# Second layer of a two-layer transformer kernel: sums loaded in halves, a half-precision slot map, the attention's queries and angles put ahead of the expert beats, the gates applied in the last additions

## The chip, the cores and the metric

The kernel runs on one core of one Trainium2 chip. The metric is the device time of one execution in microseconds. The engines are TensorE (PE, with its weight load PEld), VectorE (DVE), ScalarE (ACT), GpSimd (POOL) and the DMA queues, of which SyncE's (SP) is the main one.

## The reference

Two layers on 4 sequences of 256 tokens with 256 features (1024 tokens, 8 tiles of 128). Each layer adds its attention and its mixture of experts to the residual. The change is nearly all in the second layer:

```python
# layer 1 attention: q, k with rotary turn, then random features of the unit vectors
qp = _softmax_kernel(q, rand_matrix)      # sin and cos of angles, 16 heads
kp = _softmax_kernel(k, rand_matrix)      # 8 heads, each used twice
kv = jnp.einsum('bhsf,bhsd->bsfd', kp, v) # sum over heads h, per token s
out = jnp.einsum('bhsf,bsfd->bhsd', qp, kv)
out = out.reshape(b, s, HID)              # not transposed: heads and tokens are mixed
return out @ Wo.T + bo
# layer 1 experts: 8 experts, the best 2 for each token
top_k_weights, top_k_indices = jax.lax.top_k(gate_logits, TOP_K)
h = jax.nn.silu(h0) * h1 * combine_w[..., None]
out = jnp.einsum('bsem,emd->bsd', h, wo)
```

## The kernel before, in words

Every engine has its own program, written out by hand, and the programs meet in semaphores only. Nothing is scheduled by a tool: what stands in a row on an engine runs in that row.

The first layer ends with its attention's last projection on PE (`project`) and two arrays of expert sums in DRAM. **The seam** between the layers: SP loads the sums (`SUMS`), DVE adds them to the residual `x3` (`add_sums`), takes the statistics, POOL makes the reciprocal root (`layernorm_pool`) and DVE the normed tokens (`layernorm_dve`). PE transposes them (`turn_tokens`), and ACT copies them out (`take_tokens`).

**The routing stage.** PE computes values and router logits (`values_router`), and queries and keys (`queries_keys`, six matmul groups of 512 columns). DVE picks the best two experts (`choose_dve`), turns the queries (`rope_qk`), counts (`route_dve_slots`, with `rank_pe` on PE), and builds the slot map: which token stands in which of the 23 tiles of 128 slots (`map1_dve`, 16 matmuls in `map1_pe`, `map1_dve_end`). Once the map is there (`map_ok`), POOL gathers the tokens of a tile by indirect DMA (`gather_tile1`). Beside this PE makes the angles of the random features (`angles`, `turn_angles`), and DVE and ACT norms, turns, differences, sines and squares of them.

**The beats.** Beat i on PE (`expert1_pe`) transposes gathered tile i, multiplies tile i-2 by the experts' first matrices, transposes the hidden tile i-4 and multiplies tile i-5 by the second. ACT copies and takes the silu (`expert1_act`), DVE multiplies (`middle`), POOL writes the rows back to DRAM (`write_tile1`). Between its `middle`s DVE does the attention's heads in 24 parts: `meet(t, part)`, three parts for each of 8 tiles. SP stores each finished tile of heads and loads it back in another order.

**The tail.** PE transposes the loaded heads (`turn_heads`), ACT copies (`take_heads`), PE projects (`project1`), DVE adds (`take_project1`). Then the expert rows come back from DRAM (`load_rows1`, rows of the first choice on SP's queue, of the second on ACT's) and DVE adds them, and SP writes the result.

Waits have the form `engine.wait_ge(semaphore, count)`. `NT` is 8 tiles, `NT1` 23, `NSL` 16, `B` 4 sequences, `TPB` 2 tiles of each.

## Time and profile before

| | us |
|---|---|
| median of 3 runs (528.59 to 534.28) | 533.49 |
| the profiled execution | 531.84 |
| its span | 530.0 |
| PE busy (share of the span) | 492.1 (93%) |
| DVE busy | 357.5 (67%) |
| ACT busy | 299.6 (57%) |
| POOL busy | 303.5 (57%) |

The span counts from the first to the last instruction; the execution's own time is 1.84 us longer. A share is a mean over stages: the second layer, which the change is about, takes the last 140 us. Its stages have to be read one by one.

### The profile page before, as it was taken

To read this page: it belongs to the slowest core of one execution; us is meant where nothing else is said; L and a number is where in the kernel's file an instruction comes from. 1 tells how busy PE (TensorE), PEld (TensorE's weight loads), DVE (VectorE), ACT (ScalarE), POOL (GpSimd) and SP (SyncE) were. 2 spreads that over 40 slices of the span, in tenths; PEclk is the share of its full clock that TensorE was granted. 3 is DMA by queue.
4 is the path that set the end of the run, shared out by engine and by line. 5 is a ranking of instruction groups with operands and counts; after the bars stand their busy time and mean duration, and the time that the engine had idled before them with its cause. 6 is when DMAs were issued, how large, how long until landed. Compare 5 with 4: busy or idle time off the path is not lost. (4 is left out here: it accounts for less than half of the span.)

```text
span 530.0 us, 9787 instructions
## 1 busy us (share of the span) xinstructions
PE 492.1 (93%) x2935; PEld 356.9 (67%) x2935; DVE 357.5 (67%) x1030; ACT 299.6 (57%) x667; POOL 303.5 (57%) x231
## 2 busy tenths in 40 slices
PE   8999799989799999999999999999979979899982
PEld 7666676778577777778777778786665535466661
DVE  6999735847767475576484681615477979999645
ACT  1256076687685776765766756747312358466530
POOL 1046447887877678576686786744133065788440
PEclk9999799999899999999999999999999999999998
DMA  7991738999779978588686796863669021444437
GB/s 222 330 365 36 206 100 190 201 205 276 185 172 287 223 169 193 100 192 191 133 209 136 151 228 151 186 111 31 171 200 309 15 69 61 99 117 108 86 81 236
DMA packets 92996, 89.20 MB, mean 168 GB/s; under 512 B 28273, under 2 KB 87793, under 8 KB 92561
## 3 DMA queue, kind: packets, MB, share of 16 engines
q1 hardware_dynamic: 73440, 59.25, 38.9%
q0 software_dynamic: 17376, 27.24, 27.2%
q10 hardware_dynamic: 2128, 2.10, 1.2%
q8 instruction: 24, 0.39, 0.3%
q14 instruction: 28, 0.22, 0.1%
HBM read 65.42 MB, written 21.29 MB: 164 GB/s over the span
## 5 line engine op out<-in xcount | busy, mean ns | idle before, releaser
L987 POOL DMA_INDIRECT expert_sums<-expert_weights,token_of_slot x79 | 131.5, 1665 | 60.8 <-ACT expert_weights L1097 32.7
L979 POOL DMA_INDIRECT expert_weights<-normed_x,token_of_slot x79 | 91.1, 1153 | 40.2 <-issue 17.9
L581 PE MATMUL bank<-out_weights,expert_weights 128*128 128x256 f32 x256 | 60.2, 381 | 0.7 <-ACT expert_weights L707 0.7
L581 PEld LDWEIGHTS bank<-out_weights,expert_weights 128*128 128x128 f32 x256 | 46.5, 190 | 8.0 <-ACT expert_weights L707 1.8
L1021 PEld LDWEIGHTS bank<-expert_weights 128*128 128x128 f32 x316 | 39.4, 191 | 11.1 <-issue 7.9
L1021 PE MATMUL bank<-expert_weights 128*128 128x128 f32 x316 | 43.8, 281 | 2.6 <-DMA expert_weights<-experts_in 2.0
L1320 PE MATMUL bank<-expert_weights,tiles 128*128 x92 | 44.1, 602 | 1.3 <-DVE tiles L1370 1.3
L1284 POOL DMA_INDIRECT tiles<-normed_x,token_of_slot x23 | 27.5, 1194 | 29.8 <-DVE token_of_slot L1278 20.5
L1043 PE MATMUL bank<-expert_weights 128*128 128x256 f32 x158 | 43.2, 392 | 0.7 <-ACT expert_weights L1074 0.7
L820 DVE SCALAR_TENSOR_TENSOR expert_weights<-bank,blocks_valid 128x64 f32<-128x64 f32 x32 | 7.2, 224 | 50.3 <-ACT expert_weights L684 49.1
L1289 POOL DMA_INDIRECT expert_rows<-expert_weights,token_of_slot x23 | 30.1, 1311 | 18.9 <-ACT expert_weights L1365 14.3
L1097 ACT ACTIVATE expert_weights<-bank,chosen_bf 128x256 f32<-128x256 f32 x79 | 33.3, 474 | 9.5 <-PE bank L1050 7.9
L1081 ACT ACTIVATE expert_weights<-bank,expert_weights 128x128 f32<-128x128 f32 x79 | 25.0, 370 | 17.5 <-PE bank L1021 17.3
L538 PE MATMUL bank<-keys,expert_weights 128*128 128x112 f32 x256 | 34.7, 279 | 0.0
L995 DVE SCALAR_TENSOR_TENSOR expert_weights<-expert_weights,chosen_before_bf 128x6 f32<-128x6 f32 x79 | 15.6, 222 | 28.0 <-DMA expert_weights<-normed_x,token_of_slot 28.0
L1088 ACT ACTIVATE expert_weights<-bank,expert_weights 128x128 f32<-128x128 f32 (+1 forms) x40 | 14.9, 372 | 34.7 <-PE bank L1031 32.5
L538 PEld LDWEIGHTS bank<-keys,expert_weights 128*128 128x128 f32 x256 | 31.1, 192 | 4.3 <-issue 4.3
L573 PE MATMUL bank<-expert_weights 112*128 112x512 f32 x64 | 33.0, 602 | 0.5 <-issue 0.3
L1043 PEld LDWEIGHTS bank<-expert_weights 128*128 128x128 f32 x158 | 27.9, 194 | 8.2 <-issue 3.6
L361 POOL TENSOR_TENSOR expert_weights<-iota,block_max 128x474 f32<-128x474 f32 x8 | 9.5, 1189 | 34.8 <-DVE block_max L347 30.1
L669 ACT ACTIVATE tiles<-bank 128x512 f32<-128x512 f32 x32 | 19.2, 601 | 17.8 <-PE bank L506 17.7
L1074 ACT ACTIVATE expert_weights<-bank 128x512 f32<-128x512 f32 (+1 forms) x40 | 24.0, 600 | 7.7 <-PE bank L1010 7.7
(282 smaller groups left out, 1124.5 us busy)
## 6 DMA issues: line engine op xcount, KB each, us to landing
expert_weights<-experts_in SPq DMA_DIRECT2D x79, 177.5 KB
expert_weights<-experts_out SPq DMA_DIRECT2D x79, 128.0 KB
expert_weights<-experts_rest SPq DMA_DIRECT2D x79, 64.2 KB
expert_weights<-L_ffn_wi SPq DMA_DIRECT2D x32, 128.0 KB
expert_weights<-w_comp SPq DMA_DIRECT2D x1, 2048.0 KB, 12.0
expert_weights<-fold_g SPq DMA_DIRECT2D x1, 2048.0 KB, 15.1
expert_sums<-zeros SPq DMA_DIRECT2D x2, 1024.0 KB, 21.1
expert_weights<-L_ffn_wo SPq DMA_DIRECT2D x16, 128.0 KB
```

The lines of the kernel that those rows point to most:

```text
L538: ins = nc.tensor.matmul(ps[2][:, hg * NKEY:(hg + 1) * NKEY], QT[:, s * H * NSR + hg * P:s * H * NSR + (hg + 1) * P], kwin[:, b, i, :], st ...
L573: nc.tensor.matmul(ps[out_bank(t, s)][:, :], VW[b % 2][0:NKEY, i * D:(i + 1) * D], PTB[s % 2][0:NKEY, :], start=True, stop=True).then_inc( ...
L581: ins = nc.tensor.matmul(ps[7][:, 0:HID], AO[:, h * P:(h + 1) * P], wc3[:, h, :], start=(h == 0), stop=(h == H - 1))
L979: nc.gpsimd.indirect_dma_start(xt0[g % 4], None, xn0, bass.IndirectOffsetOnAxis(ap=MAP[:, g:g + 1], axis=0)).then_inc(gathered[g % 4], 16)
L987: nc.gpsimd.indirect_dma_start(sums0[g % 2], bass.IndirectOffsetOnAxis(ap=MAP[:, g:g + 1], axis=0), yt0[g % 4], None, compute_op=ALU.add). ...
L1021: ins = nc.tensor.matmul(ps[5][:, g % 2 * P:(g % 2 + 1) * P], w1t[g % NW][:, k * W1C:k * W1C + P], xT0[q % 2][:, c * P:(c + 1) * P], start ...
L1043: nc.tensor.matmul(ps[YBANK[g % 2]][:, HID:2 * HID], hT0[q % 2][:, g % 2 * P:(g % 2 + 1) * P], w2t[q % NPT][:, g % 2 * HID:(g % 2 + 1) * H ...
L1081: ins = nc.scalar.activation(hT0[q % 2][:, c], ps[5][:, c], ACT.Relu, bias=w1t[g % NW][:, KC * W1C:])
L1097: nc.scalar.activation(yt0[g % 4], ps[YBANK[g % 2]][:, HID:2 * HID], ACT.Copy, scale=GY[:, g:g + 1]).then_inc(y_sb, 3 - len(pair(q)))
L1284: nc.gpsimd.indirect_dma_start(xt1[g % 4], None, xn1, bass.IndirectOffsetOnAxis(ap=MAPX1[:, g:g + 1], axis=0)).then_inc(gathered[n % 4], 16)
L1289: nc.gpsimd.indirect_dma_start(rows1, bass.IndirectOffsetOnAxis(ap=MAP[:, g:g + 1], axis=0), yt1[g % 4], None).then_inc(written1[g % 4], 16)
L1320: ins = nc.tensor.matmul(ps[HB[g % 2]][:, :], xT1[g % 3][:, k * P:(k + 1) * P], w[:, 0, k * 2 * MI:(k + 1) * 2 * MI], start=(k == 0), stop ...
```

## The change

- The sums of the first layer are loaded in four halves, and the first four tiles are normed before the rest has its statistics. Transposing tokens and `values_router` alternate on PE.
- In both layers, the comparison with the chosen experts and the product with the ranks are one DVE instruction each for all tiles, where there was one for each tile.
- The slot map of layer 1 is in half precision, without the gates, and 23 columns wide. The gates now multiply in the last additions on DVE (one instruction for each tile and choice).
- The second half of queries and keys has three PSUM banks of its own, so that PE needs no `rope_qk` before it. `map1_pe` follows the first `angles`, and `map1_dve_end` is two `rope_qk` instructions earlier than it was.
- In the beats, the head parts of DVE come one beat later than before and catch up (`PARTS1`); norms and turns of the second half are spread out; sines follow a table (`SINES1`). The addition of the output bias on POOL moves from ahead of the gathers to behind the sixth.
- Heads of two sequences are transposed inside the beats (`HEADS1`). The rows of both choices are loaded on SP's queue, by sequence, in a layout in which a partition's two tiles are adjacent in DRAM.

```diff
+HEADS1 = {NT1 + 1: 0, NT1 + 3: 1}
+SINES1 = {3: 1, 6: 2, 9: 3, 12: 4, 15: 5, 17: 6, 20: 7}
+PARTS1 = [g + (g >= 16) + (g >= 20) for g in range(NT1)]
...
-                st(nc.vector.tensor_tensor(oh[:, t], bc(IOTA[:, 0:E].unsqueeze(1), [P, K, E]),
-                                           bc(tf[:, t, 0:K].unsqueeze(2), [P, K, E]), ALU.is_equal))
-            st.wait()
+            n = hi - lo
+            st.link(nc.vector.tensor_tensor(oh[:, lo:hi], bc(IOTA[:, 0:E].unsqueeze(1).unsqueeze(1), [P, n, K, E]),
...
-                st(nc.vector.tensor_tensor(pr[:, t], oh[:, t],
-                                           bc(CUM[:, t * E:(t + 1) * E].unsqueeze(1), [P, K, E]), ALU.mult))
-            st.wait()
+            st.link(nc.vector.tensor_tensor(pr, oh, bc(v3(CUM[:, 0:NT * E], NT).unsqueeze(2), [P, NT, K, E]), ALU.mult))
...
-        MA1 = WC[:, NT * HID:NT * HID + NSL * P]
-        MT1, MTG1 = AO[:, 0:NSL * NT1], AO[:, NSL * NT1:3 * NSL * NT1]
-        MTGW = AO[:, NSL * NT1:3 * NSL * NT1 + P]
...
+        MA1 = WC[:, NT * HID:NT * HID + NSL * P // 2].bitcast(F16)
+        MT1, MTK1 = AO[:, 0:NSL * NT1], AO[:, NSL * NT1:NSL * NT1 + NSL * NT1 // 2].bitcast(F16)
...
-        QKB, ANGB, VRB, HB = (3, 5, 0), (4, 6, 0, 7), (2, 4, 6), (3, 5)
+        QKB, ANGB, VRB, HB = ((3, 5, 0), (7, 4, 6)), (4, 6, 0, 7), (2, 4, 6), (3, 5)
...
-            wait(pe, qk_rp, 2 * (i - NQK + 1))
-            pe.wait_ge(x1t_sb, NT // 2 * (hf + 1))
+            pe.wait_ge(x1t_sb, NT)
+            if hf == 1:
+                if c == 0:
+                    pe.wait_ge(op_sb, NT)
+                else:
+                    pe.wait_ge(vr_ok, c + 1)
...
-                ins = nc.tensor.matmul(ps[2][:, MAPC:MAPC + P], MA1[:, j * P:(j + 1) * P], MTGW[:, j * 2 * NT1:j * 2 * NT1 + P],
+                ins = nc.tensor.matmul(ps[2][:, MAPC:MAPC + NT1], MA1[:, j * P:(j + 1) * P], MTK1[:, j * NT1:(j + 1) * NT1],
...
-                nc.scalar.activation(yt1[g % 4], ps[1][:, 0:HID], ACT.Copy, scale=GY1[:, g:g + 1]).then_inc(y_sb, 1)
+                nc.scalar.activation(yt1[g % 4], ps[1][:, 0:HID], ACT.Copy).then_inc(y_sb, 1)
...
+            for t in range(1, NT - 1):
                 turn_tokens(pe, t)
-            for t in range(NT - 1):
-                values_router(pe, t)
+                values_router(pe, t - 1)
             turn_tokens(pe, NT - 1)
+            values_router(pe, NT - 2)
+            values_router(pe, NT - 1)
             queries_keys(pe, 0, 0)
-            values_router(pe, NT - 1)
             queries_keys(pe, 0, 1)
+            rank_pe(pe, E1, ps[2], 1)
             queries_keys(pe, 0, 2)
             queries_keys(pe, 1, 0)
-            rank_pe(pe, E1, ps[2], 1)
             queries_keys(pe, 1, 1)
-            pe.wait_ge(op_sb, NT)
+            queries_keys(pe, 1, 2)
             angles(pe, 0)
-            queries_keys(pe, 1, 2)
-            pe.wait_ge(vr_ok, 3)
+            map1_pe(pe)
             turn_angles(pe, 0)
             turn_angles(pe, 1)
-            map1_pe(pe)
             angles(pe, 1)
             expert1_pe(pe, 0, {})
+            expert1_pe(pe, 1, {})
             pe.wait_ge(slots_ok, 3)
-            expert1_pe(pe, 1, {})
-            turn_angles(pe, 2)
-            turn_angles(pe, 3)
             pe.wait_ge(ld_e1, 16 * 3 * KC * E1)
             for i in range(2, NBEAT1):
                 if i % 4 == 2:
                     e = experts1(pe, i)
                 expert1_pe(pe, i, e)
-            turn_heads(pe, 0)
+                if i == 2:
+                    turn_angles(pe, 2)
+                    turn_angles(pe, 3)
+                if i in HEADS1:
+                    turn_heads(pe, HEADS1[i])
             for b in range(B):
-                if b + 1 < B - 1:
-                    turn_heads(pe, b + 1)
-                elif b == B - 1:
-                    turn_heads(pe, b)
                 project1(pe, b)
-
...
+                for k in range(K1):
+                    sp.dma_start(v3(ROWS1[k], NT)[:, b * TPB:(b + 1) * TPB, :],
+                                 rows1[k * T:(k + 1) * T, :].rearrange("(p t) d -> p t d", t=NT)[:, b * TPB:(b + 1) * TPB, :]).then_inc(sum1_ld[b], 16)
...
+            square_qk(act, 0, 0)
+            square_qk(act, 0, 1)
             act.wait_ge(gates_sub, 2)
             nc.scalar.activation(GATE[:, 0:NSL], GATE[:, 0:NSL], ACT.Exp).then_inc(gates_exp, 1)
-            square_qk(act, 1, 0)
-            square_qk(act, 1, 1)
+            square_qk(act, 0, 2)
+            for c in range(NQK):
+                square_qk(act, 1, c)
             take_angles(act, 0)
-            square_qk(act, 1, 2)
             roots(act, 0)
             take_angles(act, 1)
...
+                if i in SINES1:
+                    sines_of(act, SINES1[i])
+                if i - 1 in SINES1:
+                    squares_of(act, SINES1[i - 1])
+                if i in HEADS1:
+                    take_heads(act, HEADS1[i])
...
+        def heads_part(dve, st, t, part):
+
+            if part == 0 and 1 <= t < NT - 1:
+                differences(dve, t + 1)
+            meet(dve, st, t, part)
+            if (t, part) == (0, 2):
+                square_sums(dve, st, 1)
+            if (t, part) == (2, 0):
+                norms(dve, st, 1)
+            if (t, part) in ((2, 1), (3, 2)):
+                turns(dve, st, t)
...
+            dve.wait_ge(t_ps, NT * NG)
+            layernorm_dve(dve, st, 1, TILES1[0])
             dve.wait_ge(summed, 4)
             layernorm_stats(dve, st, TILES1[1])
-            dve.wait_ge(t_ps, NT * NG)
-            layernorm_dve(dve, st, 1, TILES1[0])
-            layernorm_dve(dve, st, 2, TILES1[1])
             take_out(dve, NT - 1)
             dve.wait_ge(op_sb, NT)
             layernorm_stats(dve, st, TILES1[2])
+            layernorm_dve(dve, st, 2, TILES1[1])
+            layernorm_dve(dve, st, 3, TILES1[2])
...
-            take_values(dve, st, 2)
+            take_logits(dve, st, 2)
             st.wait()
             choose_dve(dve, st, E1, K1, 1, VR_TILES[2])
             route_dve(dve, st, E1, K1, 1)
-            for c in range(1, NQK):
-                rope_qk(dve, 0, c)
+            take_values(dve, 1)
+            take_values(dve, 2)
+            rope_qk(dve, 0, 0)
             route_dve_slots(dve, st, E1, K1, ps[2], 1)
+            rope_qk(dve, 0, 1)
+            rope_qk(dve, 0, 2)
             map1_dve(dve, st)
-            map1_experts(dve, st)
             rope_qk(dve, 1, 0)
             rope_qk(dve, 1, 1)
+            map1_dve_end(dve, st)
+            rope_qk(dve, 1, 2)
+            map1_experts(dve, st)
             square_sums(dve, st, 0)
-            rope_qk(dve, 1, 2)
-            map1_dve_end(dve, st)
             norms(dve, st, 0)
             turns(dve, st, 0)
             differences(dve, 0)
             turns(dve, st, 1)
...
+            differences(dve, 1)
+            done = 0
+            for g in range(NT1):
+                for n in range(done, PARTS1[g]):
+                    heads_part(dve, st, n // 3, n % 3)
+                done = PARTS1[g]
+                middle(dve, g)
+            for n in range(done, 3 * NT):
+                heads_part(dve, st, n // 3, n % 3)
+
+            for b in range(B - 1):
+                take_project1(dve, b)
             for b in range(B):
-                take_project1(dve, b)
-            dve.wait_ge(ao_rd, B)
-            for b in range(B):
+                if b == 2:
+                    take_project1(dve, B - 1)
+                dve.wait_ge(ao_rd, b + 1)
                 dve.wait_ge(sum1_ld[b], 16 * K1)
-                x = X[:, b * TPB * HID:(b + 1) * TPB * HID]
                 for k in range(K1):
-                    ins = nc.vector.tensor_tensor(x, x, ROWS1[k][:, b * TPB * HID:(b + 1) * TPB * HID], ALU.add)
-                    if k == 0:
-                        ins.then_inc(part_ok, 1)
-                        dve.wait_ge(part_ok, b + 1)
-                ins.then_inc(f_ok, 1)
+                    if k:
...
+                    for t in range(b * TPB, (b + 1) * TPB):
+                        nc.vector.scalar_tensor_tensor(out=x3[:, t, :], in0=v3(ROWS1[k], NT)[:, t, :], scalar=GATE[:, t * K1 + k:t * K1 + k + 1],
+                                                       in1=x3[:, t, :], op0=ALU.mult, op1=ALU.add).then_inc(f_ok if k else part_ok, 1)
...
+                for hf in range(2):
+                    lo, hi = hf * NT // 2, (hf + 1) * NT // 2
+                    for i in range(2):
...
+                        sp.dma_start(v3(SUMS[i], NT)[:, lo:hi, :], sums0[i][lo * P:hi * P, :].rearrange("(t p) d -> p t d", p=P)).then_inc(sum_ld[i][hf], 16)
...
+                for e1 in (0, 1):
                     for k in range(KC):
                         load_expert1(e1, k)
-                for tiles in (range(NT - 1), range(NT - 1, NT)):
+                for tiles in TILES1:
                     lo, hi = tiles[0], tiles[-1] + 1
                     sp.wait_ge(xn_ok, NT + hi)
                     for k in range(K1):
-                        sp.dma_start(xn1[k * T + lo * P:k * T + hi * P, :].rearrange("(t p) d -> p t d", p=P), xn3[:, lo:hi, :]).then_inc(x1_st, 16)
+                        sp.dma_start(xn1[k * T:(k + 1) * T, :].rearrange("(p t) d -> p t d", t=NT)[:, lo:hi, :], xn3[:, lo:hi, :]).then_inc(x1_st, 16)
...
-                pool.wait_ge(xn_ok, 2 * NT)
-                pool.wait_ge(ld_s1, 16 * 5)
-                nc.gpsimd.tensor_tensor(x3, x3, bc(BO.unsqueeze(1), [P, NT, HID]), ALU.add).then_inc(bias_ok, 1)
...
+                    if i == 1:
+                        pool.wait_ge(xn_ok, 2 * NT)
+                        pool.wait_ge(ld_s1, 16 * 5)
+                        nc.gpsimd.tensor_tensor(x3, x3, bc(BO.unsqueeze(1), [P, NT, HID]), ALU.add).then_inc(bias_ok, 1)
```

Where instructions stand, at three places. First DVE, from the end of the map's comparisons to the map's end (L1253 before, L1260 now, are the comparisons `MA1`; L1185/L1186 is `rope_qk`; L1275 to L1278, now L1282 to L1284, is `map1_dve_end`; L1258 to L1261, now L1265 to L1268, `map1_experts`; L1379 `square_sums`). Before:

```order
L1261 TENSOR_SCALAR tile_expert<-expert_weights 1x23
L1185 SCALAR_TENSOR_TENSOR keys<-bank,shared_w 128x512
L1185 SCALAR_TENSOR_TENSOR expert_weights<-bank,shared_w 128x512
L1185 SCALAR_TENSOR_TENSOR keys<-bank,shared_w 128x512
L1185 SCALAR_TENSOR_TENSOR expert_weights<-bank,shared_w 128x512
L1379 TENSOR_SCALAR expert_weights<-bank 128x48 x2
L1185 SCALAR_TENSOR_TENSOR keys<-bank,shared_w 128x512
L1185 SCALAR_TENSOR_TENSOR expert_weights<-bank,shared_w 128x512
L1275 COPY block_max<-bank 128x23
L1276 SCALAR_TENSOR_TENSOR block_max<-bank,choices 128x23
L1277 SCALAR_TENSOR_TENSOR token_of_slot<-bank,block_max 128x23
L1278 TENSOR_SCALAR token_of_slot<-token_of_slot 128x23
```

and now:

```order
L1260 TENSOR_TENSOR out_weights<-iota,block_max 128x1024 x2
L1186 SCALAR_TENSOR_TENSOR keys<-bank,shared_w 128x512
L1186 SCALAR_TENSOR_TENSOR expert_weights<-bank,shared_w 128x512
L1186 SCALAR_TENSOR_TENSOR keys<-bank,shared_w 128x512
L1186 SCALAR_TENSOR_TENSOR expert_weights<-bank,shared_w 128x512
L1282 SCALAR_TENSOR_TENSOR block_max<-bank,choices 128x23
L1283 SCALAR_TENSOR_TENSOR token_of_slot<-bank,block_max 128x23
L1284 TENSOR_SCALAR token_of_slot<-token_of_slot 128x23
L1186 SCALAR_TENSOR_TENSOR keys<-bank,shared_w 128x512
L1186 SCALAR_TENSOR_TENSOR expert_weights<-bank,shared_w 128x512
L1265 TENSOR_TENSOR expert_weights<-iota,starts 1x184
```

The last of the map's instructions stood behind all `rope_qk`, `map1_experts` and `square_sums`; now it stands behind four `rope_qk` instructions of the second half.

Second PE, around the first `angles` (L1174/L1175 is `queries_keys`, L1197 to L1203, now L1198 to L1205, `angles`; L1217/L1221 `turn_angles`). Before:

```order
L396 MATMUL bank<-chosen_bf,ones_bf 128x8
L1174 MATMUL bank<-normed,expert_weights 128x512 x2
L1197 MATMUL bank<-expert_weights,qc_T 64x512 x2
L1197 MATMUL bank<-q_up_weights,qc_T 64x512 x2
L1201 MATMUL bank<-expert_weights,qc_T 64x512
L1203 MATMUL bank<-keys,qc_T 64x512
L1201 MATMUL bank<-q_up_weights,qc_T 64x512
L1203 MATMUL bank<-keys,qc_T 64x512 x2
L1174 MATMUL bank<-normed,expert_weights 128x512 x2
L1217 MATMUL bank<-ident,q_up_weights 128x128
```

and now:

```order
L395 MATMUL bank<-chosen_bf,ones_bf 128x8
L1175 MATMUL bank<-normed,expert_weights 128x512 x8
L1198 MATMUL bank<-expert_weights,qc_T 64x512 x2
L1198 MATMUL bank<-q_up_weights,qc_T 64x512 x2
L1203 MATMUL bank<-expert_weights,qc_T 64x512
L1205 MATMUL bank<-keys,qc_T 64x512
L1203 MATMUL bank<-q_up_weights,qc_T 64x512
L1205 MATMUL bank<-keys,qc_T 64x512 x2
L1274 MATMUL bank<-expert_weights,out_weights 128x23 x16
L1221 MATMUL bank<-ident,q_up_weights 128x128
```

The last two groups of `queries_keys` stood behind the rank and behind the first `angles`; now all are ahead of it, and the 16 matmuls of the map (L1274, 23 columns) follow it directly, ahead of `turn_angles`.

Third DVE, at the end (L1370/L1374 is `middle`, L1433/L1437 and L1436/L1440 are parts 1 and 2 of `meet`, L1469/L1473 `take_project1`). Before:

```order
L1370 TENSOR_TENSOR tiles<-bank,tiles 128x256
L1430 TENSOR_REDUCE shared_w<-expert_weights 128x128
L1431 TENSOR_SCALAR shared_w<-shared_w 128x128
L1370 TENSOR_TENSOR tiles<-bank,tiles 128x256
L1433 TENSOR_TENSOR out_weights<-shared_w,values 128x2048
L1436 TENSOR_REDUCE expert_weights<-out_weights 128x256
L1469 TENSOR_TENSOR residual<-bank,residual 128x512 x4
L1615 TENSOR_TENSOR residual<-residual,normed 128x512 x8
```

and now:

```order
L1434 TENSOR_REDUCE shared_w<-expert_weights 128x128
L1435 TENSOR_SCALAR shared_w<-shared_w 128x128
L1374 TENSOR_TENSOR tiles<-bank,tiles 128x256
L1437 TENSOR_TENSOR out_weights<-shared_w,values 128x2048
L1374 TENSOR_TENSOR tiles<-bank,tiles 128x256
L1440 TENSOR_REDUCE expert_weights<-out_weights 128x256
L1374 TENSOR_TENSOR tiles<-bank,tiles 128x256
L1473 TENSOR_TENSOR residual<-bank,residual 128x512 x3
L1631 SCALAR_TENSOR_TENSOR residual<-normed,gates,residual 128x256 x8
L1473 TENSOR_TENSOR residual<-bank,residual 128x512
L1631 SCALAR_TENSOR_TENSOR residual<-normed,gates,residual 128x256 x8
```

The last `middle` stood ahead of the last two head parts and now stands behind all of them; the eight additions of 512 columns are sixteen of 256 with a gate.

## Rows read from the trace of the kernel before

**Rows 1.** The chain of waits, from the last expert matmul of the beats: start, us, what.

```profile
501.44 1.73 PE bank L1320 x4
...
504.05 0.42 DVE tiles L1370
...
509.02 1.72 DMA heads<-expert_weights
510.76 0.60 SPq L1743
...
511.40 5.68 DMA out_weights<-heads
```

**Rows 2.** Timeline of DVE, the seam: start, us, instructions, idle before and releaser.

```profile
386.23 1.22 DVE L871 TENSOR_TENSOR residual<-residual,tiles 128x1024 f32<-128x1024 f32 x1 [2.46 <-DMA tiles<-expert_sums]
```

**Rows 3.** Timeline of PE, the seam.

```profile
384.66 7.17 PE L581 MATMUL bank<-out_weights,expert_weights 128*128 128x256 f32 x32 [0.69 <-ACT expert_weights L707]
393.70 0.76 PE L1121 MATMUL bank<-ident,normed 128*128 128x128 f32 x4 [1.87 <-DVE normed L418]
...
397.36 4.22 PE L1226 MATMUL bank<-shared_w,normed 128*128 128x136 f32 x28
```

**Rows 4.** Stretches: busy PE, PEld, DVE, ACT, POOL; PE's granted clock, DMA share, GB/s.

```profile
391.80:393.70 1.90, 0.04 (x1) 0.00 (x0) 1.83 (x8) 0.00 (x0) 1.24 (x2) 1.00 0.85 249
...
396.00:397.00 1.00, 0.86 (x5) 0.49 (x4) 0.82 (x3) 0.58 (x2) 0.03 (x1) 0.50 0.74 235
...
430.00:437.00 7.00, 4.99 (x21) 2.75 (x22) 4.47 (x7) 6.32 (x10) 5.08 (x5) 1.00 0.34 94
```

**Rows 5.** Timeline of DVE, the routing stage.

```profile
401.15 0.18 DVE L1235 COPY out_weights<-bank 128x24 f32<-128x24 f32 x1 [0.33 <-PE bank L1226]
...
403.20 2.28 DVE L281 CAST top_float<-top_index 128x48 f32<-128x48 uint32 x1
...
414.47 0.77 DVE L324 TENSOR_TENSOR out_weights<-out_weights 128x16 f32<-128x16 f32 x8
...
417.13 0.54 DVE L1249 TENSOR_TENSOR expert_weights<-expert_weights,gates 128x368 f32<-128x368 f32 x1
...
420.80 0.73 DVE L1185 SCALAR_TENSOR_TENSOR keys<-bank,shared_w 128x512 f32<-128x512 f32 x1
...
425.48 0.18 DVE L1278 TENSOR_SCALAR token_of_slot<-token_of_slot 128x23 int32<-128x23 int32 x1
```

**Rows 6.** Timeline of POOL, the routing stage.

```profile
400.90 4.53 POOL L1790 TENSOR_TENSOR residual<-residual,shared_w 128x2048 f32<-128x2048 f32 x1 [3.04 <-DVE normed L418]
```

**Rows 7.** Timeline of PE, the map and the second half's angles.

```profile
420.30 3.77 PE L1267 MATMUL bank<-expert_weights,out_weights 128*128 128x128 f32 x32
425.11 1.08 PE L1197 MATMUL bank<-keys,qc_T 128*64 128x512 f32 x4 [1.04 <-DVE expert_weights L1185]
```

**Rows 8.** Timeline of DVE, the beats.

```profile
437.02 0.42 DVE L1370 TENSOR_TENSOR tiles<-bank,tiles 128x256 f32<-128x256 f32 x1 [0.56 <-ACT tiles L1353]
...
458.40 0.42 DVE L1370 TENSOR_TENSOR tiles<-bank,tiles 128x256 f32<-128x256 f32 x1
458.74 2.28 DVE L1433 TENSOR_TENSOR out_weights<-shared_w,values 128x2048 f32<-128x2048 f32 x1
...
482.95 0.42 DVE L1370 TENSOR_TENSOR tiles<-bank,tiles 128x256 f32<-128x256 f32 x1
```

**Rows 9.** Timeline of DVE, the first layer's routing.

```profile
27.12 2.24 DVE L324 TENSOR_TENSOR expert_weights<-expert_weights 128x192 f32<-128x192 f32 x8
...
32.24 3.35 DVE L355 TENSOR_TENSOR expert_weights<-iota,block_max 128x768 f16<-128x768 f32 x2
```

**Rows 10.** Timeline of all engines, the tail.

```profile
510.70 0.96 POOL L1289 DMA_INDIRECT expert_rows<-expert_weights,token_of_slot  x1 [0.64 <-ACT expert_weights L1365]
...
514.26 3.30 SPq L1517 DMA_DIRECT2D normed<-expert_rows  x4
...
517.12 0.66 PE L1445 MATMUL bank<-ident,out_weights 128*128 128x128 f32 x4 [0.19 <-DMA out_weights<-heads]
...
518.46 1.99 PE L1460 MATMUL bank<-expert_weights 128*128 128x256 f32 x8 [0.69 <-ACT expert_weights L1452]
...
522.07 5.41 DVE L1615 TENSOR_TENSOR residual<-residual,normed 128x512 f32<-128x512 f32 x8 [0.88 <-DMA normed<-expert_rows]
```

129 lines of the change are left out of this document (52 added, 77 removed).

## The prediction

> **What bounds the kernel now.** I read the chain of waits first, from its end. It runs from the last expert matmul of the beats to the last `middle` (504.05), through the last head parts on DVE to 509.02, through the heads' store and load, which lands at 517.1, and from there over the projection to the last additions [rows 1, 10]. Over the whole span PE is the busiest engine, but in the second layer the stages differ. In the seam PE stands still from 391.83 to 393.70 and waits for normed tokens [rows 3]. In the routing stage DVE is busy without a gap from 401.15 to 425.66, with PE and POOL behind it: POOL's first gather waits for the map's last instruction (425.48), PE's second `angles` (425.11) for the last `rope_qk` [rows 5, 7]. In the beats DVE is busy nearly as long as PE: three beats' work with a full tile of heads takes (482.95 - 458.40)/3 = 8.18 us on DVE [rows 8], and three beats on PE take 9.06 us (3.02 each by the chain of waits: a matmul group of 1.73 [rows 1], one of 0.87, two pairs of transposes of 0.22). In the tail DVE waits, and then adds for 5.41 us [rows 10].
>
> **First layer's routing.** Eight products of 192 columns take 2.24 us [rows 9]. One of 1536 columns, at the rate of the 2048-column product (2.28 us, [rows 8]), takes 1.7: 0.5 less. The two merged comparisons save by the same rate about 0.3 each. That is 1.1 us on DVE in a row; PE has other matmuls there, so I take 0.8 us, with 0 and 1.1 as bounds.
>
> **The seam.** The last sums are there at 386.2 [rows 2]. With halves, the first four tiles need only the first half of each array, some 3.7 us earlier; their normed tokens are then ready by about 390, before PE ends the projection at 391.83 [rows 3]. What is late next is that projection itself, which the change doesn't touch. PE then alternates: two transposes (0.22 at the pace of the trace) and four `values_router` matmuls (28 take 4.22, so 0.60) [rows 3]. The logits of six tiles are there at 391.85 + 0.8 (first copy by ACT) + 6 x 0.82 = 397.5, where DVE took them at 401.15 [rows 5]: **3.6 us**. Tile 7 needs DVE's `take_out` after 391.83, statistics, and 0.9 us of POOL: ready at 394.5, in time. The stores to DRAM now stand behind 12 weight loads on SP and ahead of 24; they end near 400, and the last weight load near 411, both before the gathers and the first expert matmul.
>
> **The routing stage.** Of DVE's 24.5 us from 401.15 to the map [rows 5] these go: the CAST of 2.28 us, which is 0.18 elsewhere and ends with POOL's bias addition at 405.43 [rows 5, 6], since that addition moves: 2.1; merged comparisons and products (0.77 for eight products of 16 columns, one takes about 0.24; likewise the comparisons) 0.9; the gates' product 0.46 and a copy 0.1; `map1_experts` 0.8 and `square_sums` 0.25, which now stand behind the map; one pair of `rope_qk`, 1.32 (0.66 each in a row, [rows 5]). Sum 5.9. Half-precision comparisons cost DVE the same, as their inputs stay single; on PE the 16 map matmuls had 3.77 us [rows 7] and become 16 short ones, under 1 us, done before DVE asks. PE must have all `queries_keys` and the first `angles` done first: 391.85 + 6.6 of transposes and values + 6 x 1.73 + rank 0.4 + 4.4 = 414.0, and DVE reaches the map's end at 415.6. So the map is ready 3.6 + 5.9 = 9.5 us earlier, at 416.2.
> That isn't yet the gain, since the beats need the second `angles` ahead of them in PE's row. DVE's last `rope_qk` now ends at 416.2 + 1.3, `turn_angles` goes in front (0.4), so `angles` starts at 418.0 instead of 425.11 [rows 7]: **7.0 us**. From there to the first `middle` (437.02, [rows 8]) lie 11.9 us of PE, ACT copies, three activation tables of 1.28 us, sine and square, all in the same row as before. First `middle` at 430.0.
> PE now stands still for about 2.8 us in 414.7 to 418. After the standstill of 1.9 us in the seam the granted clock fell to 0.50, 1.2 GHz, for some 3 us; after the many short waits in 430 to 437 it stayed at 1.00 [rows 4]. By the one row `angles` and what follows become 1.5 us longer, by the other nothing; I take 0.5.
>
> **The beats.** The parts of DVE are the same work in another row, so DVE's sum is: six full tiles of 8.18, two tiles without differences 7.05 each, less one `middle` of 0.34 (23, not 24), `square_sums` 0.3, norms 1.9, turns 2 x 1.45: 68.0 us from the first `middle` to the last. PE's sum from its first expert matmul (5 us earlier) is 1.94 + 1.94 + 2.16 + 18 x 3.02 + 2.8 + 1.7 = 65: its last group ends 3 to 5 us before DVE is through. So **DVE is the bound of the beats now**, where before (437.02 to 509.0, 72 us) it waited some 5 us, partly for PE, which had waited for DVE's norms and turns in early beats. The last `middle`, which stood ahead of two head parts, stands behind them, at 430.0 + 0.5 + 68.0 + 0.7 = 499.2. The 0.7 is for POOL's bias addition, 4.53 us [rows 6], which now meets DVE's differences and turns about 425.5. Bounds: 0, since DVE waits there for the first silu anyway, and 4.5.
>
> The row shows that a conversion on DVE stood still until POOL's addition was over [rows 5, 6], while two comparisons beside POOL took 1.67 us each [rows 9] and later ones 0.95 to 1.35. The Trainium skill (SBUF — State Buffer, "Who interferes with whom") says that DVE instructions with two SBUF inputs block fully against a GpSimd instruction that reads SBUF. By that rule the differences would wait for all of it; the comparisons of the trace were slowed, not blocked for POOL's whole time. By the rule the 0.7 would be nearer to 1.5, as most of it lies under the wait for the silu.
>
> **The tail.** The last head part ends 0.35 before the last `middle` M. Store, issue and load take 8.1 us as before (509.02 to 517.12, [rows 1, 10]): M + 7.8. PE transposes (0.7), then does `project1` of the third sequence (1.8), DVE adds it (0.7): M + 11.0. DVE adds no rows before that. Meanwhile the last tile's second matmul, copy, write (2.8 us to landing) end at M + 6.3, and SP issues eight loads of 0.45. Before, the last write was issued at 510.70 and the first additions came 11.4 us later [rows 10], with ACT's four loads behind the last `take_heads`; that wait goes. Two MB at the 249 GB/s of the seam [rows 4] land by M + 16, when DVE comes to the last pair. DVE: sixteen additions of 256 columns with a gate at 0.34 to 0.36 are 5.6 us (5.41 before) and 0.7 for the last projection: M + 17.4. From the last addition to the span's end were 2.5 us: M + 19.9 (25.5 before, from 504.5). The gates cost nothing in ACT's copy and nothing more here. Bounds 18.5, and 22.5 if the first rows come 7.8 us after their issue, as they did before (514.26 to 522.07, [rows 10]).
>
> **Sum.** 499.2 + 19.9 - 0.8 = 518.3 us of span, 11.7 less than 530.0. The profiled execution is 531.84, so 520.1; from the median of 533.49 it is 521.8. I forecast 521.
>
> **Rivals.**
> (1) *The port between DVE and POOL takes it back.* The bias addition blocks DVE at a moment without cover, and POOL's gathers 6 and 7, queued behind its 4.5 us, come late to beats 6 and 7. For it: the CAST. Against: the silu's wait. Price 3 to 5 us on a DVE that is the bound: 525. Chance 0.12.
> (2) *The tail is bound by transfers.* All eight row loads stand on one queue behind the slow heads loads (3.32 us of issue, [rows 1]); before they had two queues. If they take 1 us each, the last lands at M + 19 and the end is M + 24: 525. Against: a load now has half as many runs, of twice the length. Chance 0.13.
> (3) *The change doesn't do what it says in the beats*: PE, not DVE, stays the bound, because ACT's silu follows the heads' sines late, and DVE waits 5 us as before. Then M is near 504 and the time 525.5. Chance 0.08.
> (4) *The other side.* PE's standstill before the second `angles` drops the clock to 0.50 and it doesn't come back in the beats. Each us of PE's 65 us of work then costs one more. It takes 4 us to use up PE's lead over DVE, 11.7 to use up the gain and 5.3 to be slower by 1%: it decides from 21 us of work at the lower level. At 30 us the time is 535. For it: the seam's row; against: the fall lasted 3 us there. Chance 0.03.
> (5) More than forecast: clock and port cost nothing, 2 KB runs land at once, 1.1 from the first layer: 516. Chance 0.1.
> My own forecast, 519 to 523.5, has the rest, 0.54.
>
> Range 514.5 to 527: it holds (1) to (3) and (5), and leaves out (4) and larger errors. A measurement tells 1%, 5.3 us, from no change. Faster by over 1% (under 528.2): 0.90; within: 0.07; slower: 0.03.
>
> **What the changed profile would show.** DVE takes the first logits of six tiles near 397.5; the CAST is 0.2 us; the map's last instruction near 416; second `angles` near 418, with the granted clock of the stretch; first `middle` near 430; DVE without gaps in the beats, the last `middle` near 498, behind all parts; the third projection's addition 11 us later. I am wrong if DVE waits in the beats for ACT or PE for over 3 us, if POOL's addition stretches a DVE instruction, or if rows land after DVE wants them.

## The result, and the profile after

The changed kernel takes 526.68 us (median of 20 runs, 523.2 to 530.86), the kernel before 533.76 (20 runs, 528.59 to 541.6). The ratio is 0.9887, 95% interval 0.986 to 0.9913: faster by 1.1%, 7.1 us between the medians. I had forecast 521.0, which is 12.5 under the median shown. Two later sets of runs of the same kernel, beside the kernel before, gave 0.9851 (0.979 to 0.9913) and 0.988 (0.9815 to 0.9945). The profiled execution took 525.44 us, its span 523.6: 5.3 above the forecast span.

The profile after, timeline of PE at the end of the first layer and in the seam ([rows 3] before):

```profile
388.00 7.17 PE L579 MATMUL bank<-out_weights,expert_weights 128*128 128x256 f32 x32 [0.69 <-ACT expert_weights L705]
395.01 0.60 PE L1119 MATMUL bank<-ident,normed 128*128 128x128 f32 x4
395.96 0.70 PE L1230 MATMUL bank<-shared_w,normed 128*128 128x136 f32 x4 [0.35 <-ACT normed L1124]
```

`project(7)` (L579) starts 3.3 us later than before, though the change was to bring it 0.8 forward. The standstill of 1.87 us behind it is gone; a wait of 0.35 is left. Timeline of DVE, from the seam to the map's last instruction ([rows 5] before):

```profile
400.24 0.18 DVE L1241 COPY out_weights<-bank 128x24 f32<-128x24 f32 x1 [1.37 <-PE bank L1230]
...
401.96 0.19 DVE L284 CAST top_float<-top_index 128x48 f32<-128x48 uint32 x1
...
418.95 0.18 DVE L1284 TENSOR_SCALAR token_of_slot<-token_of_slot 128x23 int32<-128x23 int32 x1
```

The CAST takes 0.19 us, not 2.28; from the first logits of six tiles to the map are 18.9 us, not 24.5. Timeline of PE, in front of the second `angles` ([rows 7] before):

```profile
416.63 0.57 PE L1274 MATMUL bank<-expert_weights,out_weights 128*128 128x23 f16 x16
418.76 0.30 PE L1221 MATMUL bank<-ident,q_up_weights 128*128 128x128 f32 x1 [1.56 <-DVE expert_weights L1186]
...
420.59 0.30 PE L1221 MATMUL bank<-ident,q_up_weights 128*128 128x128 f32 x1 [1.26 <-DVE expert_weights L1186]
...
421.09 1.08 PE L1198 MATMUL bank<-keys,qc_T 128*64 128x512 f32 x4
```

The map's 16 matmuls take 0.57 us (3.77 before). PE waits 1.56 and 1.26 us for `rope_qk`, as foreseen, and here `angles` runs at full speed (1.08 us). Timeline of DVE, the first `middle` (L1374), and the end of the beats ([rows 8] before):

```profile
432.94 0.42 DVE L1374 TENSOR_TENSOR tiles<-bank,tiles 128x256 f32<-128x256 f32 x1 [3.60 <-ACT tiles L1357]
...
498.61 2.27 DVE L1440 TENSOR_REDUCE expert_weights<-out_weights 128x256 f32<-128x2048 f32 x1
500.80 0.41 DVE L1374 TENSOR_TENSOR tiles<-bank,tiles 128x256 f32<-128x256 f32 x1
```

From the first `middle` to the last are 67.9 us. DVE is busy for 66.7 of them (60.8 of 67.0 before), with no wait before the last `middle`: DVE is the bound of the beats. Timeline of all engines, the tail ([rows 10] before):

```profile
505.49 0.97 POOL L1295 DMA_INDIRECT expert_rows<-expert_weights,token_of_slot  x1 [0.87 <-ACT expert_weights L1369]
...
508.64 3.64 SPq L1521 DMA_DIRECT2D normed<-expert_rows  x8
...
511.60 0.69 DVE L1473 TENSOR_TENSOR residual<-bank,residual 128x512 f32<-128x512 f32 x1 [2.18 <-PE bank L1464]
512.55 1.80 DVE L1631 SCALAR_TENSOR_TENSOR residual<-normed,gates,residual 128x256 f32<-128x256 f32 x4 [0.26 <-DMA normed<-expert_rows]
...
515.26 1.80 DVE L1631 SCALAR_TENSOR_TENSOR residual<-normed,gates,residual 128x256 f32<-128x256 f32 x4 [0.92 <-DMA normed<-expert_rows]
516.98 0.68 DVE L1473 TENSOR_TENSOR residual<-bank,residual 128x512 f32<-128x512 f32 x1
517.58 3.50 DVE L1631 SCALAR_TENSOR_TENSOR residual<-normed,gates,residual 128x256 f32<-128x256 f32 x8
```

The sixteen gated additions take 1.80 + 1.80 + 3.50 = 7.1 us. From the last `middle`'s end to the span's end are 22.4 us. The chain of waits of the changed kernel doesn't run over the third projection. It runs over the last write's landing and the landing of the second pair of row loads (of two loads, one for each choice):

```profile
505.49 3.02 DMA expert_rows<-expert_weights,token_of_slot
...
509.95 5.21 DMA normed<-expert_rows
...
515.26 0.89 DVE residual L1631 x2
```

### The profile page after: what moved, and what is told of

Read it like the earlier page. It is cut to its first block, busy times and chain, and to the rows that moved or that the text cites. A ratio compares the mean times of both kernels' runs of the same rounds, so it can differ in the third digit from the quotient of the medians.

```text
span 523.6 us, 9740 instructions
## 1 busy us (share of the span) xinstructions
PE 484.6 (93%) x2919; PEld 350.1 (67%) x2919; DVE 355.3 (68%) x1010; ACT 298.8 (57%) x667; POOL 301.1 (58%) x231
## 4 chain that ended last, share of the span: by engine, by line
PE 56%; DVE 25%; issue 7%; DMA 5%; ACT 3%; POOL 3%; SPq 0%; DVEq 0%; POOLq 0%; another core or an unknown queue 0%; ACTq 0%
PE bank L579 10%; PE bank L1019 6%; PE bank L536 6%; PE bank L1041 5%; PE bank L571 5%; PE bank L1048 4%; PE bank L1029 4%; DVE out_weights L1437 3%; DVE expert_weights L1440 3%; PE bank L554 3%; PE bank L1008 3%; PE bank L504 2%; PE bank L524 2%; DVE shared_w L1434 2%; DMA expert_weights<-normed_x,token_of_slot 2%
## 5 line engine op out<-in xcount | busy, mean ns | idle before, releaser
L579 PE MATMUL bank<-out_weights,expert_weights 128*128 128x256 f32 x256 | 60.2, 381 | 0.7 <-ACT expert_weights L705 0.7
L579 PEld LDWEIGHTS bank<-out_weights,expert_weights 128*128 128x128 f32 x256 | 46.5, 190 | 8.1 <-ACT expert_weights L705 1.8
L1290 POOL DMA_INDIRECT tiles<-normed_x,token_of_slot x23 | 26.2, 1141 | 30.2 <-DVE token_of_slot L1284 22.0
L1295 POOL DMA_INDIRECT expert_rows<-expert_weights,token_of_slot x23 | 28.0, 1217 | 19.9 <-ACT expert_weights L1369 16.6
L1079 ACT ACTIVATE expert_weights<-bank,expert_weights 128x128 f32<-128x128 f32 x79 | 25.0, 372 | 22.1 <-PE bank L1019 13.7
L993 DVE SCALAR_TENSOR_TENSOR expert_weights<-expert_weights,chosen_before_bf 128x6 f32<-128x6 f32 x79 | 15.6, 221 | 26.1 <-DMA expert_weights<-normed_x,token_of_slot 25.7
L1086 ACT ACTIVATE expert_weights<-bank,expert_weights 128x128 f32<-128x128 f32 (+1 forms) x40 | 14.9, 372 | 29.2 <-PE bank L1029 22.4
L667 ACT ACTIVATE tiles<-bank 128x512 f32<-128x512 f32 x32 | 19.2, 600 | 18.0 <-PE bank L504 11.7
## 6 DMA issues: line engine op xcount, KB each, us to landing
expert_weights<-w_comp SPq DMA_DIRECT2D x1, 2048.0 KB, 11.6
```

What stands on the lines that cost most here:

```text
L579: ins = nc.tensor.matmul(ps[7][:, 0:HID], AO[:, h * P:(h + 1) * P], wc3[:, h, :], start=(h == 0), stop=(h == H - 1))
L1079: ins = nc.scalar.activation(hT0[q % 2][:, c], ps[5][:, c], ACT.Relu, bias=w1t[g % NW][:, KC * W1C:])
L1290: nc.gpsimd.indirect_dma_start(xt1[g % 4], None, xn1, bass.IndirectOffsetOnAxis(ap=MAPX1[:, g:g + 1], axis=0)).then_inc(gathered[n % 4], 16)
L1295: nc.gpsimd.indirect_dma_start(rows1, bass.IndirectOffsetOnAxis(ap=MAP[:, g:g + 1], axis=0), yt1[g % 4], None).then_inc(written1[g % 4], 16)
```

## The experiments

One trace of each kernel can't tell a cause from a chance, so each trace is read in stages, cut at the start of `project(7)`, the first `middle` and the last, and the span's end. All times in us; "half clock" is the part of the first 380 us that the granted clock was missing (the sum over stretches of 10 us of ten times one less the clock).

### The two kernels as they are

The changed kernel twice more beside other runs (e5, e11), the kernel before beside such runs (e12), and last two traces of each kernel on one chip (e13 to e16):

> The changed kernel as it is, once more, beside the other runs of this job. In its first profile project(7) starts at 388.00 and the clock stays at 1.00 before the second angles; three relatives of it start project(7) at 380.0 to 381.9, and in all three the clock falls to 0.50 when PE has stood still twice (1.56 and 1.26 us) ahead of the second angles, which costs 2.7 us to the first middle. If both are chances of the single execution, this profile shows project(7) between 380 and 388 and, three times in four, 47.7 us from there to the first middle instead of 44.9.

> The changed kernel as it is, for the comparison inside this job. Ratio to the kernel before near 0.987; 46.5 to 47.9 us from project(7) to the first middle with the fall of the clock, 44.9 without.

> The kernel before as it is, for a second look at its seam. In its first profile the clock fell to 0.50 after PE's wait in the seam, and the first logits came on DVE 17.0 us after the start of project(7); with merges in the first layer alone it did not fall, and they came after 14.8. If the fall is a chance of the execution, this look shows one of the two; the routing (24 us) and the tail (25.6 to 26) are the same in either case.

> The kernel before as it is, a further look. So far three traces of it or of its relative start project(7) at 384.6, 384.7 and 393.4, with 5.1 to 6.8 us of the first layer lost to the lower clock; ten of the changed kernel and its relatives have 0 to 6.8, mostly 1.7. If the first layer is the same in both kernels and the rest is chance, these looks at before and after on one chip overlap.

> As the run before it. Of the seam: the clock falls behind PE's wait of 1.9 to 2.0 us in two of three traces; expected 52.4 us from project(7) to the first middle with the fall, 50.1 without.

> The changed kernel as it is, beside the two looks at the kernel before. Expected: the start of project(7) within the spread of those two; 44.9 us to the first middle without the fall of the clock, 46.5 to 47.9 with it.

> As the run before it: a start of project(7) within the spread of the two looks at the kernel before, and 44.9 us to the first middle without the fall of the clock, 46.5 to 47.9 with it.

| kernel, trace | half clock | start of project(7) | to first middle | to last middle | to the end |
|---|---|---|---|---|---|
| before, first profile | 5.1 | 384.66 | 52.36 | 67.03 | 25.95 |
| before, e12 | 6.8 | 393.43 | 52.43 | 67.07 | 26.67 |
| before, e13 | 5.1 | 393.16 | 49.82 | 67.10 | 25.92 |
| before, e14 | 6.8 | 396.07 | 51.78 | 67.18 | 25.87 |
| after, first profile | 1.7 | 388.00 | 44.94 | 67.86 | 22.80 |
| after, e5 | 1.7 | 386.62 | 46.55 | 67.92 | 22.31 |
| after, e11 | 1.7 | 386.27 | 47.68 | 67.66 | 22.99 |
| after, e15 | 6.8 | 395.07 | 44.92 | 68.11 | 22.30 |
| after, e16 | 5.1 | 390.23 | 46.57 | 67.69 | 22.91 |

e12's tail, 26.67, lies above the 25.6 to 26 that were expected of it; the other stages of the kernel before came as expected.

The first layer starts `project(7)` anywhere from 384.7 to 396.1 us in the kernel before and from 386.3 to 395.1 in the changed one, and on one chip the two overlap (393.2 and 396.1 before, 395.1 and 390.2 in the changed one, though e16 lies below the spread that was expected of it). No difference between the kernels can be told from this spread. It has two parts. One is the clock. Timeline of PE, kernel before, first profile, and then the changed kernel, the same twelve matmuls behind PE's waits for the first gathered tiles:

```profile
59.07 5.33 PE L2012 MATMUL bank<-shared_w,expert_weights 128*128 128x256 f32 x12
```

```profile
58.80 2.76 PE L2031 MATMUL bank<-shared_w,expert_weights 128*128 128x256 f32 x12
```

The other is waits of 1 to 2.5 us for ACT copies that were late without a releaser. Here the transposes that ACT copies were done at 201.4, ACT started at 204.31, and PE waited for the copy (second row):

```profile
204.31 0.60 ACT L1072 ACTIVATE expert_weights<-bank 128x512 f32<-128x512 f32 x1 [1.58 <-issue]
...
204.97 0.70 PE L1041 MATMUL bank<-expert_weights 128*128 128x256 f32 x2 [0.99 <-ACT expert_weights L1072]
```

What holds ACT there stays open. It isn't spread evenly over the executions, and it isn't the kernel. From 60 to 380 us ACT stands idle for over 0.9 us with no releaser 7 to 13 times in thirteen of the eighteen traces, and once or never in the other five: the kernel before's first profile and e1 to e4, which ran on one chip. PE's idle time in that stretch is 7.5 to 8.5 us in these five and 10.7 to 15.6 in the rest. So the two first profiles, 384.66 and 388.00, compare an execution of the one sort with one of the other.

Behind `project(7)` the stages are steady but for one thing, the stretch to the first `middle`. In the kernel before it is 49.8 or 51.8 to 52.4, in the changed one 44.9 or 46.5 to 47.7: it is longer where the clock fell. Stretches of the changed kernel with a fall (e5; busy PE, PEld, DVE, ACT, POOL, granted clock, DMA share, GB/s), at the second `angles`:

```profile
417.40:419.40 2.00, 0.74 (x6) 0.56 (x7) 1.93 (x6) 0.00 (x0) 1.12 (x1) 1.00 0.00 0
419.40:421.40 2.00, 2.00 (x8) 0.77 (x8) 1.49 (x5) 0.28 (x1) 1.65 (x2) 0.50 0.36 98
```

and its `angles`, 1.98 us for four matmuls where the first profile had 1.08:

```profile
417.36 0.30 PE L1221 MATMUL bank<-ident,q_up_weights 128*128 128x128 f32 x1 [1.55 <-DVE expert_weights L1186]
...
419.19 0.30 PE L1221 MATMUL bank<-ident,q_up_weights 128*128 128x128 f32 x1 [1.26 <-DVE expert_weights L1186]
419.90 1.98 PE L1198 MATMUL bank<-keys,qc_T 128*64 128x512 f32 x4
```

The waits are the same as in the first profile to 0.01 us, and the clock falls in one and not in the other. Of the changed kernel and its relatives without a filler it falls in seven of ten traces (e5, e11, e16, and below e1, e3, e4, e8; not in the first, e15 and e7) and costs 1.4 to 2.9 us.

In the kernel before the fall is in the seam, and there the waits are not the same. PE's wait for the first normed tokens, in e12 (with a fall) and in e13 (without):

```profile
402.61 0.76 PE L1121 MATMUL bank<-ident,normed 128*128 128x128 f32 x4 [2.00 <-DVE normed L418]
```

```profile
400.92 0.76 PE L1121 MATMUL bank<-ident,normed 128*128 128x128 f32 x4 [0.58 <-DVE normed L418]
```

It depends on when the second array of sums lands, 0.3 to 1.7 us after the start of `project(7)`. The clock fell behind waits of 1.57 (e14), 1.87 (first profile) and 2.00 us, and not behind 0.58 and 0.91 (e2, below).

### Filling PE's waits

```diff
             map1_pe(pe)
+            keep_busy(ps[3][:, 0:HID], 5)
             turn_angles(pe, 0)
+            keep_busy(ps[3][:, 0:HID], 4)
             turn_angles(pe, 1)
```

`keep_busy` does that many matmuls on zeros, which nobody reads. These are the counts of e6; e9 and e10 have 3 and 2. e10 also has two such matmuls ahead of each of the first two gathered tiles of the first layer, and four ahead of its first transposes of probabilities.

> The changed kernel with matmuls on zeros put into PE's two waits ahead of the second angles (five and four of 256 columns, about 1.1 and 0.9 us of the 1.56 and 1.26); their results are never read. Theory: the fall of the granted clock costs 2.7 us from the second angles to the first middle in most executions, and it needs the standstill. Then the clock stays at 1.00, project(7) to the first middle is 44.9 us, and the time is 1.5 to 2.7 us under that of the changed kernel in this job. Rival: the fall has nothing to do with the standstill, or the filler delays the transposes; then the stretch stays 47.7 us and the time is the same or up to 0.5 us longer.

> The changed kernel with two edits: matmuls on zeros, three and two (0.48 us each by the trace of the first filler, whose nine were 4.3 us and delayed the transposes by 0.8), in PE's two waits ahead of the second angles, and DVE's addition of the fourth projection ahead of the second sequence's rows, where DVE waits 0.92 us for their landing, and not ahead of the third's. Expected: no fall of the clock there, 44.9 to 45.0 us from the start of project(7) to the first middle (46.5 to 47.9 in five of seven executions without filler); the wait for the second pair of rows goes from 0.92 to 0.2 and the tail is 0.3 to 0.6 us shorter than 22.3 to 22.8. Time 1.5 to 3 us under the changed kernel of this job. Rival: the landing of the rows sets the end, and the addition moved only turns into a later wait; then the tail stays 22.3 us and only the clock's share is gained.

> As the run before it, with matmuls on zeros in the first layer as well: two ahead of each of the first two gathered tiles (PE waits 1.3 us twice) and four ahead of the first transposes of probabilities (PE waits 2.1 to 3.2 us). In the traces so far the clock falls behind one of these waits or both in seven of eight executions and takes 1.7 to 5.2 us of PE's time at half speed. If the falls come from the standstills, the clock stays at 1.00 there, project(7) starts 1.7 to 3.4 us earlier, and the time is 3 to 6 us under the changed kernel. If they come from something else, they stay, and nothing is gained over the run before.

The second edit of e9 (and of e10):

```diff
             for b in range(B):
-                if b == 2:
+                if b == 1:
                     take_project1(dve, B - 1)
```

The clock stayed at 1.00 between `project(7)` and the first `middle` in all three. e6 took 45.7 us there: its fillers are 0.48 us each and delayed the transposes by 0.8. e9 took 45.06 and e10 44.93. Timeline of PE in e9:

```profile
416.29 1.54 PE L1477 MATMUL bank<-zeros 128*128 128x256 f32 x6
417.99 0.30 PE L1221 MATMUL bank<-ident,q_up_weights 128*128 128x128 f32 x1 [0.16 <-DVE expert_weights L1186]
...
418.40 1.06 PE L1477 MATMUL bank<-zeros 128*128 128x256 f32 x4
419.82 0.30 PE L1221 MATMUL bank<-ident,q_up_weights 128*128 128x128 f32 x1 [0.36 <-DVE expert_weights L1186]
...
420.32 1.08 PE L1198 MATMUL bank<-keys,qc_T 128*64 128x512 f32 x4
```

There is no fall in three traces where seven of ten had one. With a chance of seven in ten each, three without would come up by luck once in 37 times. The seam says the same: a fall behind each of three long waits, none behind the two short ones. So the standstill is very likely needed for the fall, and it isn't sufficient. In the first layer e10 had no half clock at all, but one trace of a relative without fillers (e4) had none either, and `project(7)` started at 387.69.

One less the mean granted clock, times the span, is what each run lacked of full clock. Over six runs each it is 9.4 us for the changed kernel (e11), 6.5 for e9 and 4.8 for e10 beside it; e6 has 8.1 and e5 beside it 8.2. The times don't follow. Medians are 526.57 for e11, 528.29 for e9, 525.85 for e10. The ratios to the kernel before are 0.9854 (0.9795 to 0.9914) for e6, 0.9896 (0.9832 to 0.996) for e9 and 0.9856 (0.979 to 0.9922) for e10, beside 0.9851 (e5) and 0.988 (e11) of the changed kernel: no gain that can be told from none.

The addition moved ahead has tails of 22.42 (e9) and 22.98 (e10), inside the changed kernel's 22.3 to 23.0. Still it is worth 0.6 us. In the five traces of the changed kernel the last addition ends 5.90 or 5.91 us after the second pair of rows has landed; in e9 and e10 it ends 5.30 after. That landing itself comes anywhere from 13.4 to 14.7 us after the last `middle`, and in whole tails this hides the gain. DVE's waits for rows are 0.54 and 0.42 us in e9, 0.94 and 0.39 in e10.

### The first layer's merged instructions

e1 puts the loops back in the first layer of the changed kernel, e2 takes them out of the kernel before:

```diff
-            st.link(nc.vector.tensor_tensor(pr, oh, bc(v3(CUM[:, 0:NT * E], NT).unsqueeze(2), [P, NT, K, E]), ALU.mult))
+            for t in range(NT):
+                st(nc.vector.tensor_tensor(pr[:, t], oh[:, t],
+                                           bc(CUM[:, t * E:(t + 1) * E].unsqueeze(1), [P, K, E]), ALU.mult))
```

(and the comparison likewise; first layer only).

> The changed kernel, with the first layer's comparisons and products in loops over the tiles again, as before; the second layer keeps the merged ones. In the changed kernel's profile project(7) starts at 388.00, 3.3 us later than before, though nothing on its path was meant to be slower. Theory A (the lateness is a spread between executions, not the change): the merges are worth nothing to PE, which has other matmuls until 35 us, so the time is 526 to 527.5 and project(7) starts anywhere between 381 and 390. Theory B (the merges shift the engines into a phase with more waits in the first beats): project(7) starts near 384.7 and the time is 3 us lower, 523 to 524. Theory C, that of the prediction (the merges are worth 0.8 us): 527.5.

> The kernel before with one part of the change alone: the first layer's comparisons and products as one instruction each. Theory A (PE's other matmuls cover DVE there): the time is that of the kernel before, 533 to 534.5. Theory B (the merges bring waits into the beats of the first layer): 536 to 537, with the start of project(7) 3 us later than 384.66. Theory C (0.8 us of gain): 532.9.

e1: 521.63, ratio 0.9839 (0.979 to 0.9887), `project(7)` at 381.94. e2: 528.70 beside 528.95, ratio 0.9982 (0.9956 to 1.0008), `project(7)` at 384.57 where the first profile had 384.66. The two relatives with merges that ran beside them (e3, e4) start it at 380.0 and 380.1. The times rule out theory B for e2 (3 us more would be a ratio of 1.006), but not theory C's 0.8 us, and single starts of `project(7)` spread too far to tell it. PE's timeline decides, for theory A. DVE's merged instructions are 0.9 us shorter (two comparisons 0.96 instead of 1.17 each, the product 1.76 instead of 2.24; 1.1 forecast). But PE, busy with other matmuls, starts the first group that needs the map at 35.13 us before and at 35.02 after, and waits 0.18 in both.

### The seam: whole sums

```diff
-                for hf in range(2):
-                    lo, hi = hf * NT // 2, (hf + 1) * NT // 2
...
-                        sp.dma_start(v3(SUMS[i], NT)[:, lo:hi, :], ...).then_inc(sum_ld[i][hf], 16)
+                for i in range(2):
...
+                    sp.dma_start(v3(SUMS[i], NT), ...).then_inc(sum_ld[i][0], 16)
```

> The changed kernel with the sums of the first layer loaded as two whole arrays again, before the additions in halves. The prediction gave the seam 3.6 us and put the halves at the root of it. If so, the first normed tiles come about 3.7 us later against the start of project(7), PE stands still about 1.5 to 2 us after project(7), the first logits on DVE come 2 to 3.5 us later, and the first middle too. Rival: the order on PE alone (transposes and values in turn, statistics behind) gives most of it; then under 1 us is lost.

531.03 us, 0.9878 (0.98 to 0.9956). The first logits' `max` comes 14.59 us after the start of `project(7)`, 12.46 in the changed kernel: **2.1 us**. The first `middle` comes at 47.06, 2.12 above the 44.94 of a trace without a fall, and this one had none. Timeline of PE in e7:

```profile
399.59 0.76 PE L1119 MATMUL bank<-ident,normed 128*128 128x128 f32 x4 [0.70 <-DVE normed L417]
...
403.71 0.44 PE L1119 MATMUL bank<-ident,normed 128*128 128x128 f32 x2 [0.99 <-DVE normed L417]
```

Two waits, 1.7 us in all, for the normed tokens. In the kernel before that `max` comes at 17.05 (first profile), 17.13 (e12), 16.47 (e14) and 14.52 (e13), and at 14.84 in e2. The last two are the ones with the short waits and no fall. From 14.84 to 17.05, then, 0.96 us are the longer wait (1.87 against 0.91) and about 1.2 the clock. e7 is an execution of the short sort too (its first wait is 0.70), so 2.1 us is what the halves are worth at the least; where the sums land late, they also save the longer wait and the fall behind it.

### The bias addition back in the routing stage

```diff
+                pool.wait_ge(xn_ok, 2 * NT)
+                pool.wait_ge(ld_s1, 16 * 5)
+                nc.gpsimd.tensor_tensor(x3, x3, bc(BO.unsqueeze(1), [P, NT, HID]), ALU.add).then_inc(bias_ok, 1)
                 pool.wait_ge(map_ok, 2)
```

(and gone from beat 1).

> The changed kernel with POOL's bias addition ahead of the gathers again, where it meets the routing on DVE. By the prediction a conversion or an instruction like it on DVE is held up by 2.1 us, and the map comes about 2 us later; the 0.7 us that I gave the addition in the beats go. The stretch from project(7) to the map's last instruction is then 33 us, not 31.1, and the first middle 1.5 to 2 us later. Rival: what stands on DVE under the addition now is not held up; then nothing changes (31.1), and the beats are 0.3 us shorter.

527.11 us, 0.9867 (0.9805 to 0.9929). The map comes at 31.57 after the start of `project(7)`, not 31.1: 0.46 us later, not 2. Neither 33 nor an unchanged map was right. Timelines of POOL and DVE in e8:

```profile
397.45 4.53 POOL L1809 TENSOR_TENSOR residual<-residual,shared_w 128x2048 f32<-128x2048 f32 x1 [0.60 <-DMA normed_x<-normed]
```

```profile
399.92 0.51 DVE L279 MAX8 top<-out_weights 128x8 f32<-128x8 f32 x6
...
401.42 0.62 DVE L284 CAST top_float<-top_index 128x48 f32<-128x48 uint32 x1
```

The CAST starts at 401.42 and ends 0.06 us after POOL's addition (401.98), as in [rows 5, 6]; its price is what is left of the addition when it comes, 2.1 us before and 0.43 here. Six MAX8 beside the addition take 0.51 us, the same as without it. The Trainium skill (SBUF — State Buffer, "Who interferes with whom") says that a cast can enter a two-port mode and that whichever of DVE and GpSimd comes first then has the shared pair for its whole instruction; the trace agrees, with these two numbers. The beats are 67.92 us here and 67.66 to 68.11 with the addition in them: the 0.7 us that I gave it there can't be told from nothing.

### The tail

e3 (the gates are left out):

```diff
-                    for t in range(b * TPB, (b + 1) * TPB):
-                        nc.vector.scalar_tensor_tensor(out=x3[:, t, :], in0=v3(ROWS1[k], NT)[:, t, :], scalar=GATE[...], in1=x3[:, t, :], ...)
+                    nc.vector.tensor_tensor(x, x, ROWS1[k][:, b * TPB * HID:(b + 1) * TPB * HID], ALU.add).then_inc(f_ok if k else part_ok, 1)
```

e4:

```diff
-                load_rows1(sp)
+                load_rows1(sp, 0)
...
+            load_rows1(act, 1)
             for b in range(2, B):
                 take_heads(act, b)
```

> The changed kernel with the last additions as plain ones of 1024 columns, eight instructions for sixteen. The gates of the second layer's experts are left out, so the rows are added unweighted. In the changed kernel the sixteen gated additions take 7.1 us. If the gates and the smaller pieces are what the tail costs above the forecast, each addition of 1024 columns is as long as before (5.41 us in all) and the end comes 1.7 us earlier: 525. If the landing of the rows sets the end, DVE only waits longer between the additions, and the time stays within 0.5 us of 526.7.

> The changed kernel with the second expert's four row loads issued by ACT, ahead of its last take_heads, and the first expert's four by SP. SP issues eight loads in 3.64 us now, and DVE waits 0.26 and 0.92 us for rows between its additions. If the issue on one queue is what delays the rows, the first additions start 0.5 to 1 us earlier and do not wait: 525.5 to 526. If the bytes or the latency of the transfers set it, nothing changes: 526.7; if ACT's issues delay take_heads and with it the third projection, 527.5.

e3: 519.82, ratio 0.9848 (0.9789 to 0.9906). Its timeline of DVE:

```profile
507.64 1.42 DVE L1631 TENSOR_TENSOR residual<-residual,normed 128x512 f32<-128x512 f32 x2 [0.55 <-DMA normed<-expert_rows]
...
510.01 1.42 DVE L1631 TENSOR_TENSOR residual<-residual,normed 128x512 f32<-128x512 f32 x2 [0.95 <-DMA normed<-expert_rows]
511.34 0.68 DVE L1473 TENSOR_TENSOR residual<-bank,residual 128x512 f32<-128x512 f32 x1
512.64 2.75 DVE L1631 TENSOR_TENSOR residual<-residual,normed 128x512 f32<-128x512 f32 x4 [0.62 <-DMA normed<-expert_rows]
```

The additions are 1.5 us shorter (5.59), and the waits for rows grew from 1.18 to 2.12 us; the tail is 22.43, inside the changed kernel's 22.3 to 23.0. The whole times expected here were counted from another set of runs and can't be compared (the kernel before has 528.95 in this one); the tail can. It isn't 1.7 us shorter, and DVE waits longer, as the second theory had it. Sixteen gated pieces do cost 1.5 us more of DVE than eight plain ones (gate and smaller piece aren't told apart), but right behind them stands the landing of the rows. In e3 DVE starts on the first three pairs as they land, at 507.64, 510.01 and 512.64. Its second pair landed when that of the first profile did (13.9 us after the last `middle`), and the last addition ends 0.5 us earlier. Of the other 1.0 us, 0.4 lie ahead of that landing, and 0.6 go into the wait for the third pair.

e4: 522.11, 0.9859 (0.9816 to 0.9903), and a tail of 24.6, 1.8 longer. Two queues didn't bring the rows sooner: counted from the last `middle`, the first pair landed at 12.4 us (11.2 in the changed kernel's first profile), the second at 13.7 (13.95), the last at 16.3 (16.75). And ACT's loads stood ahead of `take_heads`:

```profile
503.78 1.80 ACTq L1520 DMA_DIRECT2D normed<-expert_rows  x4
...
505.68 1.08 ACT L1456 ACTIVATE expert_weights<-bank 128x512 f32<-128x512 f32 x2 [5.64 <-PE bank L1449]
```

so the third projection's addition came at 509.50, 13.5 us behind the last `middle`'s end, where it had been 10.4. That is its third theory, at twice the price.

## Why the prediction was wrong

The sign and most mechanisms of the second layer were right; the step that failed was the tail, in its path and in the price of its additions. The time, 521, was 5.7 below the median of 526.68, which lies just inside the upper end of my range (527).

Means over the traces of the table (four of before, five of after), against what I had put for each stage from the one profile:

| stage | forecast | measured |
|---|---|---|
| first layer | -0.8 | no difference that can be told from chance |
| project(7) to first middle | -6.5 | 51.60 to 46.13: -5.5 |
| first middle to last | +1.3 | 67.10 to 67.85: +0.75 |
| last middle to the end | -5.6 | 26.10 to 22.66: -3.4 |

The last three sum to -8.2 measured, -10.9 forecast (5.47 + 3.44 less 0.75, and 6.5 + 5.6 less 1.3, rounded). Of the 5.4 us between 12.5 forecast and 7.1 measured, 2.7 are these stages, 0.8 the first layer, and 0.8 my choice of 521 where the sum gave 11.7 us. The last 1.1 are not accounted for; they are small against the first layer's spread of 11 us between single traces. By that spread the profile after lay 5.3 above its forecast though its second layer missed by only 1.2.

**First layer's routing (0.8): failed.** "PE has other matmuls there, so I take 0.8" was half a thought. They cover all but 0.1 of it (PE at 35.13 and 35.02). My lower bound, 0, was the answer, and PE's timeline of before held it.

**The seam (3.6): right, on an incomplete ground.** The mechanism is right: the standstill is gone, and tile 7 is in time. From the start of `project(7)` to the first `max` it is 16.29 us before (mean of four) and 12.46 after, 3.8 less. But 401.15 was a time out of an execution with late sums and a fallen clock; [rows 3, 4] showed both, and I took it for the kernel's own. Against the executions with early sums and no fall it is 2.1 (e13) and 2.4 (e2), and e7 has the halves at 2.1.

**The routing stage (5.9): nearly right.** From the logits of six tiles to the map 24.51 before and 18.89 after, 5.6. The CAST's 2.1 us went, as said. (PE's way to the map adds up to 413.6 there, not 414.0, which changes nothing: DVE was later in any case.) The map in half precision and the product for all tiles did what was said.

**The clock term (0.5): mis-sized.** I had both rows, a fall and none, and took 0.5 between 0 and 1.5. It is 0 in three and 1.4 to 2.9 in seven of ten traces. In the five traces of the changed kernel it adds 1.2 on average over 44.93: 0.7 more than forecast. The kernel before is 0.8 shorter on average there than in its first profile, since e13 had no fall. These two are what the stretch to the first `middle` lacks of its forecast, less 0.4 that came better. Rival (4), a lower clock that stays, did not come: the fall was over ahead of the first `middle`.

**The beats: right.** DVE is the bound, 67.9 us between the `middle`s against 68.3. The 0.7 of the bias addition can't be seen: the addition (429.05 to 433.75) lies mostly in the 3.6 us in which DVE waits for the first silu, so there was hardly an instruction for it to hold up.

**The tail (M + 19.9): the step that failed most**, by 2.2 to 2.5 us. The forecast ran over the third projection, M + 11.0, and then over additions without a wait. The third projection's addition does end there (M + 11.1, with M = 501.21), but the path is another one. The last write lands at M + 7.3 (508.51), not M + 6.3; the second pair of rows lands at M + 13.95; from there 12 gated additions and the last projection take 5.9, and the end follows 2.6 later. "Two MB ... land by M + 16, when DVE comes to the last pair" looked at the last pair alone, which did land in time (M + 16.75; DVE came to it later). It was the first two that DVE waited for, 0.26 and 0.92 us. The other term is the price: a gated addition takes 0.44 us, not 0.35, as I had priced an instruction with three operands and a scalar by a plain one. That is 1.5 us over sixteen. Together 2.7 us, of which 0.2 came back between the instructions.

"The gates cost nothing more here" is wrong for DVE by 1.5 us, of which 0.5 reached the end (e3): without them the third pair is late. M + 22.4 is my upper bound, 22.5, for another reason: the first pair came 3.8 us after the first issue, not 7.8. Rival (2), the tail bound by transfers, was half right: the rows' landing is on the path, but not at 1 us each. The loads were issued at 0.45 us and the pairs landed at M + 11.2, 13.95, 15.5 and 16.75, and in e3 at M + 11.6, 13.9, 16.6 and 17.9. "If rows land after DVE wants them", my own sign of being wrong, came true.

**Rivals (1) and (3)** did not come: POOL's addition stretches no instruction of weight where it stands now, and in the beats DVE is busy for 66.3 of 67.5 us (433.5 to 501). That POOL is harmless isn't shown, though, only that it met little. And one row was misread. I called the two comparisons of 1.67 us in [rows 9] "slowed, not blocked for POOL's whole time". Taken one by one in that trace, POOL is at work from 32.14 to 33.11 and from 33.08 to 34.77, and the comparisons run from 32.24 to 33.93 and from 33.85 to 35.58. Each ends 0.8 us after the other engine's, and such a comparison takes 0.95 us where POOL stands still: this fits two engines that wait for each other's whole instruction and take turns.

## What to carry to other kernels

A single profile is one draw: before a stage's length goes into a sum, look at its granted clock and at the landings that it waits for, and price a fall or a late landing by itself. A gain on an engine is worth the gap that it leaves on the engine that sets the end: look there for the wait that it should shorten (0.18 us here), ahead of any multiplication. Where two resources end a tail within a microsecond of each other, as the additions and the landing of the rows here, shortening one alone buys a part: 0.5 of 1.5 us in e3. And a gain of half a microsecond is looked for behind the event that starts the stage (the landing), not in the whole stage, where the spread of that event hides it.

## What was not expected of the hardware

- The granted clock can go two ways with the same program and the same waits: behind waits of 1.53 to 1.64 and 1.26 us it fell to 0.50 in seven of ten traces and stayed at 1.00 in three. The first profile and e16 have the very same waits, 1.56 and 1.26 us, and went the two ways. With matmuls on zeros in the waits it stayed in three of three. In the seam of the kernel before it fell behind 1.57, 1.87 and 2.00 us and stayed behind 0.58 and 0.91.
- A CAST on DVE beside POOL's addition lasts until that is over, while six MAX8 at the same place are not slowed (0.51 us).
- ACT starts copies 1 to 2 us late, with no releaser that the trace shows and at other places in each execution: 7 to 13 times in thirteen traces, once or never in five, of which four ran on one chip. The cause is open.
